# A vision-transformer tower on one core: V's bias, half of the keys and the patch casts change engines in the first half

## The reference, cut to what matters

```python
h = tok(x)                       # patches @ tokW + tokb
h = h + attn0(layernorm(h))      # qkv = h @ qkv_w.T + qkv_b; 16 heads of 16; per head only the
                                 # 25 keys with the highest routing score are kept; softmax; @ v
h = h + ffn0(layernorm(h))       # softmax gate, top 2 of 8 experts, and a shared silu FFN
h = h + attn1(layernorm(h))      # causal, polynomial in place of softmax
h = h + ffn1(layernorm(h))       # ternary weights, gelu
```

## Time and profile before

| what | value |
|---|---|
| median of three runs | 953.96 us (951.94 to 956.42) |
| the profiled execution: its own time | 949.92 us |
| the profiled execution: span | 948.0 us |
| TensorE busy | 775.9 us (82%) |
| VectorE busy | 655.9 us (69%) |
| ScalarE busy | 390.5 us (41%) |
| GpSimd busy | 114.4 us (12%) |
| prologue / seven slots of the first half / the rest | 0 to 62 / 62 to 440 / 440 to 948 us |

### The profile page before, as it was taken

The page is one execution under the profiler, slowest core; times in us unless marked ns, Lnnn a source line. Parts: engine busy times, 40 slices in busy tenths (PEclk is TensorE's granted clock), DMA queues, the critical chain, the costliest instruction groups (busy, mean ns, idle before and its releaser), DMA issues.

```text
span 948.0 us, 23223 instructions
## 1 busy us (share of the span) xinstructions
PE 775.9 (82%) x9703; PEld 544.6 (57%) x9703; DVE 655.9 (69%) x1471; ACT 390.5 (41%) x552; POOL 114.4 (12%) x76
## 2 busy tenths in 40 slices
PE   3669788897979788897678779999898989899956
PEld 2446465655546564655447448577575757575634
DVE  6457778586776858688768648596868678383742
ACT  3233332423333232333233274664839283554622
POOL 0030211312030031210001001010100001010000
PEclk9969999999999999998595689999999999998968
DMA  8051010201001010020000000000000000000000
GB/s 296 1 174 48 1 66 0 66 0 66 0 2 65 0 66 0 0 88 1 1 1 1 2 1 6 20 0 22 0 22 0 22 1 24 2 1 24 2 23 23
DMA packets 6779, 26.97 MB, mean 28 GB/s; under 512 B 2256, under 2 KB 3152, under 8 KB 5072
## 3 DMA queue, kind: packets, MB, share of 16 engines
q1 hardware_dynamic: 6736, 26.35, 7.5%
HBM read 22.15 MB, written 4.19 MB: 28 GB/s over the span
## 4 chain that ended last, share of the span: by engine, by line
PE 40%; issue 24%; DVE 22%; ACT 7%; POOL 6%; DMA 1%; DVEq 0%; POOLq 0%; SPq 0%; ACTq 0%
PE PS L304 8%; PE PS L687 5%; PE PS L332 5%; PE PS L652 3%; POOL w_s L1021 3%; PE PS L629 3%; PE PS L322 3%; DVE kM L1155 2%; PE PS L675 2%; PE PS L430 2%; PE PS L665 2%; PE PS L546 2%; DVE xn L1124 2%; PE PS L623 2%; POOL rstd L1005 2%
## 5 line engine op out<-in xcount | busy, mean ns | idle before, releaser
L304 PE MATMUL PS<-tokW_h,w_s 128*128 128x256 f16 x576 | 72.2, 289 | 27.0 <-DVE w_s L1299 16.4
L665 PE MATMUL PS<-xT,wqkv_h 128*128 128x512 f16 x256 | 70.8, 431 | 23.9 <-ACT w_s L930 22.1
L811 ACT ACTIVATE Pm<-Pm 128x1024 f32<-128x1024 f32 x32 | 33.9, 1058 | 135.5 <-DVE Pm L1225 135.5
L304 PEld LDWEIGHTS PS<-tokW_h,w_s 128*128 128x128 f16 x576 | 58.4, 103 | 38.1 <-issue 28.4
L1005 POOL TENSOR_TENSOR rstd<-ve,mhalf 128x4 f32<-128x4 f32 x24 | 28.0, 1168 | 363.1 <-DVE ve L1120 363.1
L1558 DVE TENSOR_TENSOR work<-w_s,work 128x512 f16<-128x512 f32 x48 | 32.5, 690 | 47.5 <-ACT work L932 47.5
L665 PEld LDWEIGHTS PS<-xT,wqkv_h 128*128 128x128 f16 x256 | 25.2, 107 | 64.5 <-ACT w_s L930 32.5
L322 PE MATMUL PS<-ident_s,xn 128*128 128x128 f32 x256 | 45.6, 303 | 15.6 <-DVE xn L1124 14.9
L818 ACT ACTIVATE PT<-PS 128x512 f32<-128x512 f32 x64 | 37.6, 595 | 44.0 <-PE PS L420 43.8
L332 PE MATMUL PS<-xT,wat_h 128*128 128x512 f16 x192 | 48.5, 415 | 7.6 <-DVE xT L1494 7.6
L1021 POOL TENSOR_TENSOR w_s<-work,w_s 128x1536 f16<-128x1536 f32 x14 | 43.1, 3102 | 94.0 <-ACT w_s L842 94.0
(11 more groups left out here) (237 smaller groups left out, 1672.8 us busy)
## 6 DMA issues: line engine op xcount, KB each, us to landing
work<-in_x SPq DMA_DIRECT2D x8, 1536.0 KB, 6.4
out<-H SPq DMA_DIRECT2D x8, 512.0 KB, 2.6
w_s<-in_w SPq DMA_DIRECT2D x3, 1024.0 KB, 6.8
wup_s<-in_wup SPq DMA_DIRECT2D x1, 1024.0 KB, 5.2
wdn_s<-in_wdn SPq DMA_DIRECT2D x1, 1024.0 KB, 7.2
w_s<-in_tokW SPq DMA_DIRECT2D x1, 768.0 KB, 7.5
wup_s<-in_wqkv SPq DMA_DIRECT2D x1, 768.0 KB, 8.1
wdn_s<-in_s SPq DMA_DIRECT2D x3, 256.0 KB, 6.1
```

What stands on the lines that cost most here:

```text
L304: m = pe.matmul(dst, halves_[xi][:, k, rows], w[:, wi, k, cols], start=(n == 0), stop=(n == 3 * chunks - 1))
L665: m = pe.matmul(PS[:, UP_BANKS[f % 4], :], wup_h[:, c, f * P:(f + 1) * P], part[:, c, :], start=(k == 0), stop=(k == 2 * C - 1))
```

## The change

- V's bias is no longer added by VectorE. Two more matmuls for each image (16 for each group) add it in PSUM: their stationary operand `bv_rows` has ones in rows 0 and 32 and zeros elsewhere, their moving operand `bv_h` holds the bias's high part in row 0 and its low part in row 32. What is left of `values_to_blocks` is a copy, and ScalarE makes it (4 instructions, in `a_A2` after `x4_high`).
- Of the keys, chunk 0 stays on VectorE (2 instructions), chunk 1 goes to ScalarE (2 instructions, a new semaphore `k1_out`, in `a_A2` after the second tanh and before `x4_high`). `scores(g, 0)` waits for `k1_out` too.
- `high_patches` moves from the head of the slot to the place after `a_A4`, before `exps(i+1, 0)`, one group ahead: slot i now casts group i+2. The cast of group 1 moves before `exps(0, 0)` of the prologue. ScalarE's last slot is written out behind its loop.
- `low_patches` moves from GpSimd to VectorE, to the head of its slot, ahead of `attend(i, 0)`.
- The setup gets six more instructions on VectorE.

```diff
-SETUP_V = 9 + IMGS + 4
+SETUP_V = 9 + IMGS + 10
@@ TensorE, image_values(j)
-                                      start=(n == 0), stop=(n == 3 * C - 1))
+                                      start=(n == 0), stop=False)
+                for e in range(2):
+                    m = pe.matmul(PS[e * L:(e + 1) * L, 2 + j // 4, (j % 4) * P:(j % 4 + 1) * P], bv_rows[:, :],
+                                  bv_h[:, :].rearrange("p (h e d) -> p e h d", e=2, d=HD)[:, e, :, :],
+                                  start=False, stop=True)
@@ TensorE, scores(g, 0)
                     pe.wait_ge(q_out, 2 * g + 2)
+                    pe.wait_ge(k1_out, 2 * g + 2)
@@ ScalarE, a_A2
                 act.activation(t2[:, :], sg1[:, :], ACT.Tanh, scale=0.5).then_inc(rt2, 1)
+                act.wait_ge(k_mm, 2 * g + 2)
+                for e in range(2):
+                    act.activation(kM[:, 1, e, :], PS[:, 1, :], ACT.Identity, bias=bkp[:, e:e + 1],
+                                   scale=par_s[:, e:e + 1]).then_inc(k1_out, 1)
                 last_x4()
+                for n in range(2):
+                    act.wait_ge(v_mm, 8 * g + 4 * n + 4)
+                    for e in range(2):
+                        r = slice(e * L, (e + 1) * L)
+                        act.activation(Vb[r, 4 * n:4 * n + 4, :, e, 0:HD],
+                                       PS[r, 2 + n, :].rearrange("p (j hp d) -> p j hp d", j=4, d=HD), ACT.Copy)\
+                           .then_inc(v_out, 1)
@@ ScalarE, the loop
-            exps(0, 0)
-            with act.Fori(0, LAST) as i:
-                high_patches(i + 1)
+            def slot_A(i, more):
                 turns(i, 0)
                 exps(i, 1)
                 turns(i, 1)
                 a_A2(i + 1, lambda: x4_high(i))
                 a_A4(i)
+                if more:
+                    high_patches(i + 2)
                 exps(i + 1, 0)
+            high_patches(1)
+            exps(0, 0)
+            with act.Fori(0, LAST - 1) as i:
+                slot_A(i, True)
+            slot_A(LAST - 1, False)
@@ GpSimd, the loop
             with pool.Fori(0, LAST) as i:
-                low_patches(i + 1)
@@ VectorE, setup_A
-                dve.tensor_scalar(bv_s[:, :], bv_s[:, :], WS, None, ALU.mult).then_inc(setup_v, 1)
+                dve.tensor_scalar(bv_h[:, :], bv_s[:, :], WS, None, ALU.mult).then_inc(setup_v, 1)
+                dve.memset(bv_rows[:, :], 0.0).then_inc(setup_v, 1)
+                dve.wait_ge(setup_v, 9 + IMGS + 4)
+                dve.scalar_tensor_tensor(out=bv_h[32:64, :], in0=bv_s[32:64, :], scalar=WS, in1=bv_h[32:64, :],
+                                         op0=ALU.mult, op1=ALU.subtract).then_inc(setup_v, 1)
+                for r in (0, 32):
+                    dve.memset(bv_rows[r:r + 1, :], 1.0).then_inc(setup_v, 1)
+                for e in range(2):
+                    dve.tensor_scalar(bkp[:, e:e + 1], bqk_s[:, 3:4], par_s[:, e:e + 1], None, ALU.mult)\
+                       .then_inc(setup_v, 1)
@@ VectorE, keys_in and slot_in
-                for c in range(C):
-                    dve.wait_ge(k_mm, 2 * g + c + 1)
-                    ...
+                dve.wait_ge(k_mm, 2 * g + 1)
+                for e in range(2):
+                    dve.tensor_scalar(kM[:, 0, e, :], PS[:, 0, :], bqk_s[:, 2:3],
+                                      par_s[:, e:e + 1], ALU.add, ALU.mult).then_inc(k_out, 1)
-            def values_to_blocks(g):
-                ...
                 top_keys(g, last_x4)
-                values_to_blocks(g)
@@ VectorE, the loop
             with dve.Fori(0, LAST) as i:
+                low_patches(i + 1)
                 attend(i, 0)
```

More of the change, by code:

```diff
@@ L74, in build @@
         tokW_h = split_weights("tokW_h", KP, E); tokb_s = sb("tokb_s", [P, E])
-        wqkv_h = split_weights("wqkv_h", C, 3 * E); bqk_s = sb("bqk_s", [P, 4]); bv_s = sb("bv_s", [P, E])
+        wqkv_h = split_weights("wqkv_h", C, 3 * E); bqk_s = sb("bqk_s", [P, 4]); bkp = sb("bkp", [P, 2])
+        bv_h = sb("bv_h", [P, E], F16); bv_rows = sb("bv_rows", [P, L], F16)
         rW1_h = split_weights("rW1_h", C, 64); rb1_s = sb("rb1_s", [64, 1])
@@ L187, in build @@
         F = Pm
+        bv_s = Pm[:, 0, 0:E]
         relu_s = (th, hs)
@@ L215, in build @@
         k_out, keep_ok, lg_ok, lin_ok, loaded_A, loaded_B = sems("k_out keep_ok lg_ok lin_ok loaded_A loaded_B")
+        k1_out = sem("k1_out")
         loaded_embed, loaded_experts, loaded_wat, low_w = sems("loaded_embed loaded_experts loaded_wat low_w")
@@ L1016, in _ @@
             pool.wait_ge(setup_v, 7)
[L1017 to L1022, removed]
             p_rstd(ve1_ok, 1, ve, rstd, rstd1_ok)
@@ L1151, in keys_in @@
             def keys_in(g):
-                for c in range(C):
-                    dve.wait_ge(k_mm, 2 * g + c + 1)
-                    for e in range(2):
-                        dve.tensor_scalar(kM[:, c, e, :], PS[:, c, :], bqk_s[:, 2 + c:3 + c],
-                                          par_s[:, e:e + 1], ALU.add, ALU.mult).then_inc(k_out, 1)
+                dve.wait_ge(k_mm, 2 * g + 1)
+                for e in range(2):
+                    dve.tensor_scalar(kM[:, 0, e, :], PS[:, 0, :], bqk_s[:, 2:3],
+                                      par_s[:, e:e + 1], ALU.add, ALU.mult).then_inc(k_out, 1)
             def router_sigmoid(g):
@@ L1291, in slot_in, with low_patches @@
                 top_keys(g, last_x4)
-                values_to_blocks(g)
             dve.wait_ge(loaded_embed, 16 * len(loads_embed))
             low_weights(0, 1)
[L1296 to L1299, removed]
+            def low_patches(g):
+                for k in range(2):
+                    ks = slice(k * KP // 2, (k + 1) * KP // 2)
+                    dve.wait_ge(p_hi_ok, 2 * g + k + 1)
+                    dve.tensor_tensor(p_lo[:, ks, :], patch[:, ks, :], p_hi[:, ks, :], ALU.subtract).then_inc(p_lo_ok, 1)
+            low_patches(0)
             setup_A()
```

## The result

The changed kernel takes 913.04 us (median of four, 911.5 to 915.1) against 955.06 for the kernel before on the same chip: ratio 0.957 (0.953 to 0.960), 38 to 45 us less. On another chip the ratio was 0.959 (0.956 to 0.961), 913.5 against 952.2.

A forecast was written before the change was run, and what follows sets the result against it. No engine was full; slots were round trips, with TensorE waiting for GpSimd at the head and VectorE binding the tail. 13.4 + 13.4 + 1.6 = 28.4 us off the median 953.96 gave 925.6, range 915 to 940.

The forecast's parts named there:

- Tail, 7 x 1.91: Slot's last stage, keys to softmax: with work off VectorE the softmax pair starts 1.91 us earlier per slot, 13.4 us.
- the walk: Tail followed engine by engine with one slot's profiled times, giving 1.91 us a slot where VectorE alone would give 4.3.
- their twins: Similar instructions in the second half that lent ScalarE's new tail work its durations: 0.59 per V copy, 0.68 per key.
- Rivals A and C: A, tail: TensorE or ScalarE late, 935.8, chance 0.15; C, tail: V's copies on ScalarE too slow, 962, chance 0.03.
- Head, 13.4: Slot's first stage: TensorE's waits for GpSimd (10.6 us) and for ScalarE's transpose copies (2.8) go, 13.4 us over seven slots.
- The cover left at the head: VectorE's idle time remaining at the slot's head after taking the low halves: 2.3 us, about 0.9 in longer slots.
- one fall in each slot, as before: All seven slots: TensorE's clock still drops to 1.2 GHz once per slot, so no gain was counted.
- Rival B: Slots: clock falls vanish, 10.5 us more, 915.1, chance 0.10; or come twice per slot, 936.1, chance 0.06.
- the pause before 219.70 stays: End of the tail: TensorE's 2.18 us stand before the scores remains and decides the clock's fall.
- Prologue, 1.6: Before the slots: TensorE's first scores wait for the mask instead of V's blocks, ending at 48.7 not 50.29, 1.6 us.
- the median stands 4.04 us above that execution: Whole kernel: the distance from profiled execution to median before was kept, turning 921.5 into 925.6 us.

The follow-up runs named there:

- e2: Only the patches' edits (casts and low halves in their new places) against the kernel before: 932.8 us, ratio 0.980.
- f1: The kernel before plus 16 matmuls per slot that compute nothing, filling TensorE's 2.18 us stand before scores(i, 1): 956.4 us, ratio 1.004.
- f3: The patches' edits alone on the kernel before, plus the 16 filling matmuls before scores(i, 1): 927.1 us, ratio 0.973.
- f2: The changed kernel plus the 16 filling matmuls before scores(i, 1) in each slot: 912.6 us.
- b2: The kernel before, unchanged, measured and profiled a second time: 954.12 us.
- a2: The changed kernel, with nothing altered, measured and profiled a second time: 913.5 us.
- g1: The changed kernel with VectorE's `lg` behind its first instruction on the FFN's tanh, not ahead of it: 916.3 us.
- e3: The changed kernel with the patches' low halves back on GpSimd, behind its mask, one group ahead: 939.8 us, ratio 0.987.

## Why the forecast was wrong

The direction and the mechanism of both parts were right, and the time was 13 us too long. In the profiled executions the miss is 37.4 - 28.4 = 9.0 us.

- **Tail, 7 x 1.91.** Measured 16.68 - 14.56 = 2.12 a slot, 1.5 us more in all. Three terms of the walk were off by a little. TensorE's stretch from the keys to the FFN's products is 240.48 - 234.54 = 5.94 us, before it was 204.49 - 197.91 = 6.58, a gain of 0.64 where the walk had 0.46. VectorE's work from `lg` to the softmax, which "stays" at 5.25, takes 249.10 - 243.99 = 5.11, another 0.14. Against them, `lg` starts 0.16 us after the gate's modelled end of 243.83 and not 0.06, which takes 0.1 back. Of TensorE's 0.18, half is the bias product, 0.22 us for eight matmuls (V's first half takes 237.77 - 236.09 = 1.68 start to start, 1.46 before) and not 0.26, twice in a slot; the other half is that I let the products start at V's modelled end, about 0.1 late. V's copies took 0.61 each and the keys 0.76, against 0.59 and 0.68 from their twins. Rivals A and C did not come: neither TensorE's scores nor the tanh was late (the tanh waits 1.12 us for TensorE, not for V).
- **Head, 13.4.** The waits went as said, and low halves and casts cost nothing. `e2` alone shows slots with a fall 53.3 - 51.8 = 1.5 shorter (1.3 said). The cover left at the head was 1.14 us, where 2.3 and "about 0.9" were said.
- **The clock, "one fall in each slot, as before".** This is the step that failed. Rival B described it, priced it (1.5 us a fall, measured 1.2 to 1.5) and got 0.10. The argument was that "the pause before 219.70 stays" and decides, for the falls in the embedding too. The fall of the longer slot does not belong to that pause: it begins at 229.1 (the window from 229 to 230 reads 0.53), 9 us behind it and 0.6 us behind the end of the stand of 2.05 us at the embedding. The pause stayed, but it makes a fall in only some slots: two of the six later ones in the first profile of the changed kernel, two in the second. With no fall behind the scores, the kernel before always had the stand of 2.05 us at the embedding to take it, and that stand is the one the change takes away (`f1` shows the two as alternatives, `f3` and `f2` that without both there is none in the six later slots). Worth 6.0 us in four slots; another 0.6 in the first slot, whose fall was shorter, and 0.4 in the slots that kept one.
- **Prologue, 1.6.** Measured 59.58 - 57.41 = 2.2.
- **From the profiled execution to the median.** Of the 13 us some 4 are here. I carried "the median stands 4.04 us above that execution" to the changed kernel. The distance was no property of the program: the profiled execution of before had the short second half and a short last slot, `b2` had neither, and the median of the changed kernel stands 0.6 above its profiled execution (in `a2` 0.3 below it). Comparing medians, the change is worth 42 us on the first chip and 39 on the second.

The sum of the parts, 1.5 + 6.0 + 0.6 + 0.4 + 0.6 + 0.3 (second half), is 9.4; the heads' 13.4 from the grouped rows was 0.4 more than the slots' own waits add up to.

That a range ended at 915.0 with B at 915.1 is the second error: B was taken as the end, with the tail at its upper bound of 1.91 by argument and none of the other terms at their good ends.

## What to carry to other kernels

When an edit removes waits of TensorE, list all its stands of about 2 us in the period. Removing one can hand its fall to another, as in every later slot of `f1`, or lose it in part of the slots, as in four of six in the changed kernel; with none left no fall came in the six later slots of three kernels. And ask what a fall costs where it lies: nothing where TensorE waits for another engine right behind it, here 1.2 to 1.5 us where it does not. Before moving work from or to GpSimd, look at what VectorE runs beside it that reads two SBUF operands or casts there. And don't carry the distance between one profiled execution and the median over to the next kernel; profile each twice.

## What the runs showed of the hardware that I had not expected

- A slot that is shorter can run slower as a whole: `g1` has 0.22 us less in each slot without a fall, but four falls in the later slots instead of two. Its seven slots take 344.4 us together, against 343.3 and 343.0 in the two profiles of the changed kernel; its median is 2.8 us longer on the same chip, of which the slots are 1.4 in the profiles.
- The untouched second half lasts 510 or 512 us with identical instructions, and the two kinds differ in how long the clock is at 1.2 GHz in its first 66 us (26 to 36 us against 37 to 41). A difference under 3 us between two such executions says nothing about the edit.
- An fp32 to fp16 cast of VectorE, 0.43 us alone, took 2.58 us beside a GpSimd subtraction that reads SBUF (`e3`).
